# Contracting attention over head and key in chunks of 128 rows, with wider score products, folded routing weights and position rows added by the gather

## What is computed

```python
# 1: token layer, additive attention
x = emb[tokens] * sqrt(128) + positional_encoding(96, 128)
q, k, v = x @ Wq + bq, x @ Wk + bk, x @ Wv + bv
scores = einsum('d,bijd->bij', attn_scale, tanh(q[:, :, None, :] + k[:, None, :, :]))
x = layer_norm(x + softmax(scores) @ v @ Wo + bo, g1, beta1)
x = layer_norm(x + relu(x @ W1 + bf1) @ W2 + bf2, g2, beta2)
# 2: causal attention, 8 heads of 128
q, k, v = (x @ W.T for W in (Wq, Wk, Wv))        # q and k / 128**0.25
out = concat_heads(softmax(where(causal, q k^T, -inf)) @ v) @ Wo.T
# 3: mixture of 64 experts, 2 per row
h = ln(x, ln1_g, ln1_b)
probs = softmax(h @ Wr @ codebook.T / 0.7);  vals, idx = top_k(probs, 2)
moe = sum over the two of vals / sum(vals) * (silu(h @ W1[e] + b1[e]) @ W2[e] + b2[e])
shared = 0.25 * (silu(h @ Ws1 + bs1) @ Ws2 + bs2)
# then a last feed-forward with its own norm and residuals
```

## Time and profile before

| | us |
|---|---|
| three runs | 848.84, 845.55, 848.45 |
| median | 848.45 |
| the profiled execution | 848.4 |
| its span, first to last instruction | 846.6 |
| TensorE, VectorE, ScalarE, GpSimd busy | 777.9, 635.7, 625.8, 415.4 |
| qT of pair 0, of pair 4, of pair 15 written at | 12.2, 119.9, 482.6 |
| expert table ready at | about 611 |

### The profile page before, as it was taken

One profiled execution on the slowest core, in us unless ns is written; L12 is line 12 of the kernel. 1 busy time (PEld: TensorE's weight loads), 2 busy tenths in 40 slices (PEclk: granted clock), 3 DMA queues, 4 the chain that ended last, 5 costly groups with the idle time before them and its releaser, 6 DMA issues.

```text
span 846.6 us, 21646 instructions
## 1 busy us (share of the span) xinstructions
PE 777.9 (92%) x7299; PEld 603.6 (71%) x7299; DVE 635.7 (75%) x1656; ACT 625.8 (74%) x1455; POOL 415.4 (49%) x525
## 2 busy tenths in 40 slices
PE   2686999999999999999999999997689899999898
PEld 1355676676766766766766667765579899999787
DVE  4899999999999999999999995453333345433685
ACT  3686999998998989989989997554245465555354
POOL 3111133566566565575665555678425455555211
PEclk9897999999999999999999999998799999999999
DMA  5998000000000000000000000001189999995411
GB/s 100 246 204 185 3 7 9 15 19 20 16 24 18 16 24 21 16 23 22 16 22 19 17 18 18 18 22 29 34 294 394 377 396 398 318 360 212 156 31 38
DMA packets 53874, 88.34 MB, mean 104 GB/s; under 512 B 8516, under 2 KB 35227, under 8 KB 53776
## 3 DMA queue, kind: packets, MB, share of 16 engines
q1 hardware_dynamic: 35680, 71.35, 26.5%
q0 software_dynamic: 7584, 10.89, 4.7%
q10 hardware_dynamic: 10512, 4.83, 2.1%
HBM read 63.95 MB, written 25.23 MB: 105 GB/s over the span
## 4 chain that ended last, share of the span: by engine, by line
PE 47%; DVE 29%; issue 10%; DMA 4%; POOL 3%; SPq 2%; ACT 2%; POOLq 0%; DVEq 0%; ACTq 0%
DVE arena L948 15%; PE big L1680 6%; PE b_s L1368 6%; PE b_o L1522 5%; PE big L1480 4%; DMA arena<-in_wpack 3%; PE b_qk L1691 3%; PE b_s L1691 3%; PE big L1736 3%; PE big L1508 2%; PE b_s L1749 2%; DVE mx L1074 1%; PE big L1501 1%; PE b_qk L1749 1%; DVE stat_h L990 1%
## 5 line engine op out<-in xcount | busy, mean ns | idle before, releaser
L948 DVE TENSOR_TENSOR arena<-qT,b_qk 128x2304 f32<-128x2304 f32 x128 | 322.6, 2535 | 0.2
L696 ACT ACTIVATE arena<-arena 128x2304 f32<-128x2304 f32 x128 | 269.9, 2124 | 14.3 <-DVE arena L948 14.2
L1368 PE MATMUL b_s<-arena,apad 128*32 128x192 f32 x3072 | 156.2, 339 | 13.7 <-ACT arena L696 9.0
L855 ACT ACTIVATE act_h<-big,arena 128x128 f32<-128x128 f32 x324 | 92.7, 369 | 73.1 <-PE big L1680 73.1
L1368 PEld LDWEIGHTS b_s<-arena,apad 128*32 128x32 f32 x3072 | 89.1, 112 | 77.0 <-issue 38.9
L664 POOL DMA_INDIRECT eo_dram<-gT,toff x81 | 79.9, 987 | 93.1 <-DVE gT L1253 88.0
L575 POOL TENSOR_TENSOR kept<-kept,rs 96x384 f32<-96x384 f32 x64 | 55.5, 867 | 102.9 <-DVE rs L1080 102.7
L761 ACT ACTIVATE kept<-big,mx 96x96 f32<-96x96 f32 x256 | 82.8, 335 | 21.2 <-DVE mx L1074 21.0
L1680 PE MATMUL big<-hbT,arena 128*128 128x128 f32 x648 | 87.4, 278 | 6.7 <-DMA arena<-in_wpack 5.2
L1680 PEld LDWEIGHTS big<-hbT,arena 128*128 128x128 f32 x648 | 79.6, 194 | 8.2 <-issue 7.4
L1242 DVE TENSOR_SCALAR hbT<-b_t,cols 128x128 f32<-128x128 f32 x81 | 33.1, 409 | 64.1 <-PE b_t L1673 64.1
(11 more groups left out here) (213 smaller groups left out, 1477.3 us busy)
## 6 DMA issues: line engine op xcount, KB each, us to landing
arena<-in_wpack SPq DMA_DIRECT2D x81, 578.0 KB, 9.8
rows_dram<-act_h SPq DMA_DIRECT2D x1, 10320.0 KB, 55.0
prT<-rows_dram ACTq DMA_DIRECT2D x73, 64.5 KB
arena<-eo_dram SPq DMA_DIRECT2D x4, 512.0 KB, 7.6
x_dram<-res SPq DMA_DIRECT2D x16, 96.0 KB, 1.8
out<-of SPq DMA_DIRECT2D x12, 128.0 KB, 1.8
eo_dram<-gT,toff POOLq DMA_INDIRECT x81, 5.6
rows_dram<-rows_now,slots POOLq DMA_INDIRECT x64, 2.3
```

Source lines behind the costliest of these rows:

```text
L696: act.activation(v, v, ACT.Tanh).then_inc(s["tanh"], 1)
L855: last = act.activation(act_h[:, i, c * TILE:(c + 1) * TILE], big[i][:, c * TILE:(c + 1) * TILE], ACT.Silu, bias=wslot[:, slot, 2 * DFF + ...
L948: dve.tensor_tensor(ring[c % TRING].rearrange("p (x m n) -> p x m n", m=CQ, n=N), qv.unsqueeze(3).to_broadcast([D, SPLIT * QG, CQ, N]), kv ...
L1368: last = pe.matmul(b_s[32 * a:32 * a + 32, 0:SPLIT * N], apad[:, 31 - line:63 - line], t[:, :, a, m, :], start=(line == 0), stop=(line == ...
```

## The change

Six things are changed together.

- The second attention's probabilities of 4 heads (384 columns of head and key) are turned as 3 blocks of 128 instead of 4 of 96, and `attend2` contracts 128 rows of head and key at a time. For this `heads_v` writes its values so that the partition is the running number of head and key: 24 products of 32 tokens by 256 columns into four strips, in three stages instead of four products of 512 columns in four stages.
- SPLIT goes from 2 to 3 and CQ from 3 to 2: a score product has 288 columns instead of 192, and a chunk has 8 products instead of 12. The chunk of 2304 columns stays.
- Router and codebook are multiplied once (wrc), so `router` and `rT_copy` fall away.
- The position rows are divided by sqrt(128) and loaded by SP into the pair's own buffer of a ring of three (`place`); the gather adds the embedding rows to them in the DMA (`compute_op=ALU.add`), `x_rows` falls away, and the scaling goes into ScalarE's copy of the turn, into wvo, v_bias and the epsilon of the first norm. Where the first two pairs were gathered at the start, now only the first is; the others follow in the body before their own.
- The feed-forward works on x1 plus the second bias alone (x1T falls away), its first bias is corrected once for it, and the identity product in `ffn2` is a transposition. The ranks' first product is in bf16.
- `gaps` moves from `route` to `chosen`.

```diff
-SPLIT = 2
+SPLIT = 3
-CQ = 3
+CQ = 2
+PK = H // 2 * N // 128
-EARLY = 2
+EMBS = 3
...
@@ SP
+            def place(p):
+                if p >= EMBS:
+                    sp.wait_ge(s["kept"], p - EMBS + 1)
+                load(emb[:, p % EMBS, :, :], io["pe"], s[f"place{p % EMBS}"])
+            place(0)
             load(ident[:, :], io["ident"], s["ld_a"])
-            load(pe_rows[:, :], io["pe"], s["ld_a"])
...
             load(cols[:, :], io["cols"], s["ld_a"])
+            place(1)
+            place(2)
             sp.wait_ge(s["emb0"], 16 * G)
...
             sp.dma_start(rows_dram[PAGES * TILE:, :], zeros[:, 0:DC]).then_inc(s["filled"], 16)
...
-            store_x(0)
-            with sp.Fori(1, PAIRS) as p:
+            for p in range(EMBS, PAIRS):
+                place(p)
+                if p >= EMBS + 4:
+                    store_x(p - EMBS - 4)
+            for p in range(PAIRS - EMBS - 4, PAIRS):
                 store_x(p)
@@ GpSimd
+            def gather_emb(p, g):
+                pool.wait_ge(s[f"place{p % EMBS}"], 16 * (p // EMBS + 1))
+                b = p * G + g
                 pool.indirect_dma_start(
+                    emb[:, p % EMBS, g, :], None, io["L0_tok_emb"],
+                    bass.IndirectOffsetOnAxis(ap=eidx[:, b:b + 1].bitcast(U32), axis=0),
+                    bounds_check=VOCAB - 1, oob_is_err=True, compute_op=ALU.add).then_inc(s[f"emb{p % EMBS}"], 16)
...
-            for p in range(EARLY):
-                for g in range(G):
-                    b = p * G + g
-                    gather_rows(res[0:N, p, g, :], eidx[:, b:b + 1], s[f"emb{p}"])
+            gather_emb(0, 0)
+            gather_emb(0, 1)
...
             def keep_x(p):
                 if p == 0:
                     pool.wait_ge(s["setup"], 1)
-                pool.wait_ge(s["xs"], p + 1)
-                pool.tensor_tensor(pair_of(res, p), xs[:, :, :], v_bias[:, :].unsqueeze(1).to_broadcast([N, G, D]),
-                                   ALU.add).then_inc(s["kept"], 1)
+                pool.wait_ge(s["xs_t"], p + 1)
+                pool.tensor_tensor(pair_of(res, p), emb[:, p % EMBS, :, :],
+                                   v_bias[:, :].unsqueeze(1).to_broadcast([N, G, D]), ALU.add).then_inc(s["kept"], 1)
...
             def body(n):
                 at(n, 0, keep_x)
-                at(n, -1, gather_emb, 0)
+                at(n, -1, gather_next, 0)
                 at(n, 4, normalise, 3)
                 at(n, 2, root, "x1")
@@ ScalarE
             def x1T_affine(p):
...
-                act.activation(x1T[:, :], b_t[:, 0:TN], ACT.Identity, bias=beta1, scale=g1).then_inc(s["x1T"], 1)
...
             def products(p):
...
+                act.wait_ge(s["raw_mm"], 5)
+                act.activation(wrc[:, :], big[0][:, 0:E], ACT.Identity)
+                act.activation(nbf, big[0][:, E:E + FC], ACT.Identity, scale=-1.0).then_inc(s["raw_ev"], 1)
+                act.wait_ge(s["raw_ev"], 5)
+                for c in range(FC):
+                    act.activation(bf1f2[:, c:c + 1], nbf[:, c:c + 1], ACT.Identity, bias=bf1[:, c:c + 1])
...
-                at(n, 4, vv_copy, 3)
-                at(n, 5, rT_copy)
@@ VectorE
-            def x_rows(p):
...
             def route(p):
...
-                dve.tensor_tensor(gaps[:, p * G:(p + 1) * G], top[:, :, 1], top[:, :, 0], ALU.subtract)
             def chosen(p):
...
+                dve.tensor_tensor(gaps[:, p * G:(p + 1) * G], top[:, :, 1], top[:, :, 0], ALU.subtract)
...
-                at(n, 0, x_rows)
@@ TensorE
             def xs_turn(p):
...
-                pe.wait_ge(s["xs"], p + 1)
+                pe.wait_ge(s[f"emb{p % EMBS}"], 16 * G * (p // EMBS + 1))
...
             def heads_v(p, k):
...
-                g = k // 2
-                pe.matmul(dst[0:N, :], xaT[:, g * N:(g + 1) * N],
-                          vo[:, (k % 2) * 512:(k % 2 + 1) * 512], start=True, stop=True).then_inc(s["hv"], 1)
+                if k == 1:
+                    parts = [(g, 2) for g in range(G)]
+                else:
+                    parts = [(k // 2, c) for c in range(2)]
+                for i, (g, c) in enumerate(parts):
+                    for q in range(4):
+                        h, b = divmod(4 * c + q, N // 32)
+                        last = pe.matmul(dst[32 * q:32 * q + 32, i * 2 * D:(i + 1) * 2 * D],
+                                         xaT[:, g * N + 32 * b:g * N + 32 * b + 32], vo_heads[:, :, h, :],
+                                         start=True, stop=True)
+                last.then_inc(s["hv"], 1)
...
             def pr_turn(p, k):
...
-                for j in range(4):
-                    last = pe.transpose(dst[0:N, j * N:(j + 1) * N], pr[:, 4 * k + j, :], ident[0:N, 0:N])
+                for c in range(PK):
+                    first = 4 * k * N + c * 128
+                    last = pe.transpose(dst[:, c * N:(c + 1) * N], pr_flat[:, first:first + 128], ident[0:N, 0:N])
...
             def attend2(p, k):
...
-                for h in range((k % 2) * 4, (k % 2) * 4 + 4):
-                    last = pe.matmul(p_o[:, g, :], prT[:, g * H + h, :], vv[:, g, h * D:(h + 1) * D],
-                                     start=False, stop=(k == 3 and h == H - 1))
+                for c in range(PK):
+                    last = pe.matmul(p_o[:, g, :], prT[:, k, c, :], vv[:, g, c, k % 2, :],
+                                     start=False, stop=(k == 3 and c == PK - 1))
...
-            def router(p):
...
             def logits(p):
...
-                    last = pe.matmul(p_lg[:, g, :], rT[:, g * N:(g + 1) * N], cbT[:, :], start=True, stop=True)
+                    last = pe.matmul(p_lg[:, g, :], hall[:, p, g * N:(g + 1) * N], wrc[:, :], start=True, stop=True)
```

More of the change, by code:

```diff
@@ L78 @@
 YA_ORDER = [
-    (3, "ffn2"), (2, "attend1"), (5, "router"), (5, "logits"), (1, "v_rows"), (5, "ranks"),
+    (3, "ffn2"), (2, "attend1"), (5, "logits"), (1, "v_rows"), (5, "ranks"),
 ]
@@ L215, in program @@
         x1h = sb("x1h", [N, G, D])
-        x1T = sb("x1T", [D, TN])
         hid = sb("hid", [D, FC, TN])
@@ L305, in program @@
             "ids", "ld_a", "ld_b", "late", "consts", "gate", "pool_c", "setup_mm", "setup",
-            "raw_mm", "raw_ev", "emb0", "emb1", "emb2", "xs", "kept", "xs_t", "qk", "queries", "add", "tanh", "score",
[1 row of a table removed]
+            "raw_mm", "raw_ev", "kept", *[f"{n}{i}" for n in ("place", "emb") for i in range(EMBS)], "xs_t", "qk", "queries", "add", "tanh", "score",
[1 row of a table added]
             "h0_rows", "xa", "xa_t", "hg", "hv", "s2", "rs2", "pn",
[1 row of a table removed]
[1 row of a table added]
             "hot", "ohs", "cum", "oh", "rank_ps", "slot", "tid", "scat", "ahead", "gap_e", "chain",
@@ L424, in _ @@
             load(mask[:, :], io["mask"], s["late"])
-            load(wr[:, :], io["L0_ffn_Wr"], s["late"])
+            load(wrT[:, :], io["WrT"], s["late"])
             load(cbT[:, :], io["cbT"], s["late"])
@@ L639, in body @@
                 at(n, 5, counted)
-                at(n, -1, gather_emb, 1)
+                at(n, -1, gather_next, 1)
                 at(n, 5, keep_rows)
@@ L749, in vv_copy @@
             def vv_copy(p, k):
-                wait(act, s["att2"], 4 * p - 3 + k)
-                act.wait_ge(s["hv"], 4 * p + k + 1)
-                act.activation(vv[:, k // 2, (k % 2) * 512:(k % 2 + 1) * 512],
-                               bank(p, f"heads_v {k}")[0:N, :], ACT.Identity)\
+                wait(act, s["att2"], 4 * p - 2 + k if k < 2 else 4 * p)
+                act.wait_ge(s["hv"], 3 * p + k + 1)
+                if k == 1:
+                    dst = vv[:, :, 2, :, :]
+                else:
+                    dst = vv[:, k // 2, 0:2, :, :]
+                act.activation(dst.rearrange("p g a d -> p g (a d)"),
+                               bank(p, f"heads_v {k}")[:, :].rearrange("p (g n) -> p g n", g=2), ACT.Identity)\
                     .then_inc(big_read(p, f"heads_v {k}")[0], 1)
@@ L971, in setup @@
                 dve.tensor_scalar(bs2q[:, :], rows["bs2"][:, :], SHARED, None, ALU.mult)
-                dve.tensor_copy(wvo[:, :], big[0][:, 0:D])
-                dve.tensor_tensor(v_bias[:, :], big[0][0:N, D:2 * D], row["bo"][:, :], ALU.add)\
-                    .then_inc(s["setup"], 1)
+                dve.tensor_scalar(wvo[:, :], big[0][:, 0:D], 1.0 / ROOT_D, None, ALU.mult)
+                ch.link(dve.tensor_tensor(v_bias[:, :], big[0][0:N, D:2 * D], row["bo"][:, :], ALU.add))
+                ch.wait()
+                dve.tensor_scalar(v_bias[:, :], v_bias[:, :], 1.0 / ROOT_D, None, ALU.mult).then_inc(s["setup"], 1)
             def softmax1_max(p):
@@ L1423, in products @@
                     last.then_inc(s["raw_mm"], 1)
+                pe.wait_ge(s["raw_ev"], 1)
+                for c in range(FC):
+                    pe.matmul(big[0][:, E + c:E + c + 1], w1[:, c * D:(c + 1) * D], bf2, start=True, stop=True)
```

(7 more changed lines are left out.)

97 lines of the change are left out of this document (44 added, 53 removed), and 6 rows, old and new, of tables (BIG_ORDER, s).

## The result

The changed kernel takes 854.44 us (median of 5 runs, 852.62 to 857.12) against 848.29 us of the kernel before (median of 5): 1.0093 times as long, 95% interval 1.0069 to 1.0117. The profiled execution of after took 852.62 us with a span of 850.7, that of before 848.4 with 846.6. Slower, as forecast, and inside the range, but by 6.2 us at the median and 4.2 between the two profiled executions, where the forecast had 16.3. Most of the difference lies in one term of the sum, the steady pairs.

The account below looks back on a forecast made before the run. VectorE and TensorE were both taken as full in steady pairs. 848.4 + 28.3 (stall) + 0.5 (pair 2) - 0.9 (pair 3) - 7.1 (steady pairs) - 4.5 (drain) = 864.7 us, range 852 to 875.

Parts of the forecast that it names:

- The stall: Start: position rows of pair 3 land behind the clearing on SP's queue, delaying qT of pair 2 by 28.3 us.
- Rival 1: Start: position rows of pair 3 pass the clearing, queries(2) only +9.5 us, 845.9 us in all; chance 0.06.
- the smaller delays: Start: pair 1's later gather (qT about 45) and the fold's extra small work cost nothing beside the +28.3 us.
- The steady pair: Pairs 4 to 14: VectorE alone becomes the bound, a pair falls from 33.04 to about 32.4, -7.1 us over 11 pairs.
- the hole: Before qT in a steady pair: VectorE idle 0.85 us, which a faster TensorE was said not to shorten.
- VectorE's own work: Steady pair: x_rows gone, gaps moved, maximum over more columns; in all -0.65 us a pair.
- TensorE's relief: Steady pair: attend2, heads_v, scores, turns and small products save about 4 us, 32.6 to 28.6.
- Rival 2: Pairs and drain: less waiting behind GpSimd, pairs -16 instead of -7.1, drain -8, 852 or 851 us; chance 0.12.
- Rival 3: Steady pairs: TensorE becomes the bound, heads_v strips not overlapping (about 935) or 1.2 GHz level (872 to 880); chance 0.10 together.
- Pair 2: Start: TensorE comes out of 20 us of idleness at the 1.2 GHz level, +0.5 us on 29.66.
- The drain: After the last query: bound by TensorE in large part, -4.5 us, between -2 and -8.

Follow-up runs that it names:

- e3: Changed kernel with the position rows of pair 3 alone issued from GpSimd's queue instead of SyncE's: 840.94 us, 0.9919 of the kernel before.
- e9: Changed kernel with root of pair 0 moved ahead of the waiting gather of pair 3 on GpSimd: 843.46 us, 0.9958 of the kernel before.
- e4: Kernel before with half of the products of attend2 left out: 836.38 us, steady pair 32.5 us against 33.04.
- e5: Kernel before with only gaps moved from route to chosen: 847.67 us, steady pair 33.03 us against 33.04.
- e1: Changed kernel with five embedding buffers instead of three: 840.59 us, 0.9905 of the kernel before.

## What the prediction had right, and where it failed

**The stall, right.** qT of pair 2 was forecast at 87.9 and came at 87.7, by the steps forecast: place 3 issued at 66.46 (64.2 at the earliest), landed by 84.85 (85.3), gather, root, x1_norm at 87.11. e3 and e9 show both links, the queue and what stands behind the gather. Rival 1 (the rows pass the clearing) is out: on SyncE's own queue they don't.

**That the smaller delays vanish in it, right, and it hid them.** The late gather of pair 1 (12.2 us at qT of pair 2) and the fold (3.4 us) cost nothing while place 3 was later still. I put x1_norm of pair 0 without the stall at about 67; in e9 it came at 72.39, and qT of pair 2 behind it at 75.53. As 87.7 lies beyond that, the term held; for a mended kernel the reading would have been wrong by 5 us or more.

**The steady pair, wrong, by one sentence.** Forecast were -7.1 us for pairs 4 to 14, and -16.6 were measured. "TensorE is already waiting when the last addition ends, so a faster TensorE doesn't shorten this." In a steady pair it wasn't so. The last addition of the earlier trace rows ends at about 315.5. TensorE then, in the kernel before:

```profile
315.31 1.18 PE L1368 MATMUL b_s<-arena,apad 128*32 128x192 f32 x24
316.42 0.59 PE L1390 MATMUL b_qk<-xT,wqk 128*128 128x192 f32 x2
```

It is at the scores of a chunk until 316.42 and goes into the key product without idle time. Where I had seen it wait for the addition was pair 2, in the thin pipeline of the start:

```profile
58.57 0.59 PE L1390 MATMUL b_qk<-xT,wqk 128*128 128x192 f32 x2 [2.30 <-DVE arena L948]
```

So the hole belonged to TensorE, and TensorE was relieved by 2.5 us; e4, which relieves TensorE alone, closes it too. The price of the error is the hole, 8.6 of the 9.5 us by which pairs 4 to 14 were missed.

**VectorE's own work, right.** 0.67 us a pair against 0.65, ScalarE 1.41 against 1.4. But that moving gaps pays 0.46 a pair while the hole stays rested on the same wrong sentence: if TensorE waited for the last addition, an earlier addition would mean an earlier qT. On the kernel with the hole it brings nothing (e5). That gaps would cost 0.46 again without the hole was wrong too; it costs 0.07. The bound that I named, -1.5 a pair if the hole closes too (-16), was the answer.

**TensorE's relief, half.** 2.5 us instead of 4: over the eleven pairs the scores brought 0.1 where I took 0.6, attend2 0.86 instead of 1.15, the turns 0.4 instead of 0.5, heads_v its 0.9, and the small products what is left, some 0.3 instead of 0.9. It didn't matter for the sign of the step.

**Rival 2** gave 851 to 852 us and is nearest to the 852.62 of the profiled execution, but for another reason than the one it named: in the eleven pairs no wait of VectorE for GpSimd is listed before or after; a wait of VectorE for TensorE went. **Rival 3** is out for heads_v (3.2 us); its other half, the 1.2 GHz level in steady pairs, did turn up, in three pairs of e1. Pair 2 got shorter by 1.0 us in spite of TensorE's lower clock (0.80), where I had taken +0.5. The drain came out as forecast, at -4.5.

## What to carry to other kernels

Before saying that an idle time will stay, look in the stretch itself at what its releaser was doing just before: if it ran without a break up to the release, the idle time belongs to it and goes when it gets faster. A steady state with two full engines is a round with a segment on each, and the price of an edit is what it adds to its segment: the same instruction cost 0 us in one of these kernels and 0.48 us a pair in the other, the same busy time 0.14 or 1.16. A small DMA that an early stage needs must not be issued behind a large one on the same queue, and a wait is priced by what stands behind it on its engine, so undoing the one stall that shows can give back half: here 13 of 28 us, and two other delays lay under it.

## What the runs showed of the hardware

A gather that adds onto what is there holds GpSimd for 1.5 us where the plain one held it for 1.0, and lands 3.6 us after its issue where the plain one took 3.0 (medians). The 10 MB clearing held SyncE not at its own issue but at the next: 0.71 us for the clearing, 37.13 for the 64.5 KB behind it. Scores of 288 columns a product and of 192 a product took TensorE as long for the same columns, 9.4 and 9.5 us a pair.
